# The ends of a state-space scan loop: two of four step-size tiles made inside the loop, and a new order at the loop's first and last pairs

## The chip, the cores and the metric

The kernel runs on one NeuronCore of a Trainium2 chip. The metric is device time in microseconds. Engines are named as in the profile: PE is TensorE (PEld its weight loads), DVE is VectorE, ACT is ScalarE, POOL is GpSimd, SP issues the DMAs.

## The reference, cut to what matters

The reference is a small network of four layers on an input of 2 x 16 x 16 tokens with 64 channels. Each layer is a mixer and a mixture of experts. The change touches only the first layer's mixer, a four-directional selective scan over 256 positions (SEQ) in each of two images:

```python
delta = jax.nn.softplus(dts + dt_b[:, None, :, None])      # step sizes, 4 directions x 128 channels
A = -jnp.exp(A_logs)
def step(h, inp):                                          # 16 states a channel
    dt, bt, ct, ut = inp
    h = jnp.exp(dt[..., None] * A) * h + (dt * ut)[..., None] * bt[:, None, :]
    return (h, jnp.einsum('bdn,bn->bd', h, ct))
# ys of the 4 directions (rows, rows reversed, columns, columns reversed) + Dv * u are summed
y = y * jax.nn.silu(z);  return y @ out_proj_w
```

Behind it come a layer norm, the experts, a neighbourhood attention, an involution and so on, which the change leaves alone.

## The kernel before, in words

The kernel is written by hand for each engine: five instruction streams, in a fixed order, that meet at semaphores. Nothing is scheduled by a planner; an engine that waits holds up all that stands behind in its stream.

**Tiles.** A tile k (0 to 3) is one direction: 128 channels x 512 positions (both images). Channel states are laid out 8 channels x 16 states on 128 partitions, so a direction has 16 such tiles, worked as 8 pairs; the loop runs over 32 pairs (PAIRS), pair i being of direction i // 8. One pair is 128 partitions x 1024 float32.

**Step sizes of tile k.** `dts(k)` (PE, L749) multiplies the input by the folded weights into PSUM bank k. ACT takes Abs, Exp(-|x|) and Relu of it (L540 to L543). The softplus is then relu + log(1 + z), with the log made in two parts, above and below a bound: DVE's `bounded` (three tensor_scalar, L1312, L1316, L1321), ACT's log (L520), `lost` (L354) and `log1p` (L360) on POOL (tile 0's log1p on DVE), `small_log` (L1333; for tile 0 two instructions, L1337 and L1339, for the others one behind ACT's `square`, L525), `delta_log` (L1347), `delta` (L1353) and `delta_u` (delta times u, L345).

**A pair i in the loop.**
- PE: `spread_delta(i)` (L811) spreads delta over the 16 states into decay banks 0 and 1 or 2 and 3; `spread_input(i)` (L817) spreads delta x u into banks 4 and 5. Both use 32 rows of the array at a time. `spread_ahead(i + 1)` in iteration i waits for times-B of i + 1 and for scan i - 1, then does `spread_delta(i + 1)` and `spread_input(i + 2)`.
- ACT: `decays(i)` (L536), two exponentials in place in PSUM.
- DVE: `times_b(i)` (L1378), banks 4 and 5 times B into `states[i % 4]`, and the scan (L1391). The order is times-B 0, then in iteration i times-B i + 1, scan i, and after it the small steps for coming tiles.
- POOL: `hc(i)`, states times C (L452), for all pairs but the last, which DVE makes (L1412).
- PE: `sum_states(q)` (L841) sums the states of pairs 2q and 2q + 1 into bank 6, in iterations 3, 5, and so on behind the spreads.

B and C of a direction are made by `bc_mm` (PE, L754) into bank 7 and `bc_copy` (ACT, L516). `bias_blocks` (L789) are small matmuls for the next stage, in iterations 22 to 25.

**Ahead of the loop** PE does dts 0 and 1, the reversal of the input (`rev`, L759), `bc_mm(0)`, dts 2 and 3, the skip term into bank 6 (`d_mix`, L768), `bc_mm(1)`, four warming matmuls on zeros (L703), then the first spreads. ACT prepares all four tiles there, with pair 0's decays between tiles 2 and 3.

**Behind the loop** PE does six warming matmuls and the last state sum; DVE gates bank 6 (L1418) and the projection follows.

The SP queue holds the loads of weights and is not touched.

## Time and profile before

| | us |
|---|---|
| median of 3 runs | 340.89 |
| lowest, highest run | 339.46, 342.68 |
| profiled execution: span from first to last instruction | 344.4 |
| busy in that span: PE, DVE, ACT, POOL | 279.1, 249.1, 152.3, 128.5 |
| mean granted TensorE clock | 0.857 |

The profiled execution is one execution of its own, and its span is somewhat longer than the timed runs; of its own time only the span is known. All positions below are microseconds from the start of the span. Matmuls of float32 appear as two instructions each. The granted clock is 1.00 at 2.4 GHz and 0.50 at 1.2 GHz. What stands in square brackets behind a row is the idle time of the engine just ahead of it and what ended it.

### The profile page before, as it was taken

The page shows a single profiled execution, that of the slowest core. Times are in us where ns is not written, and L with a number is a line of the kernel's source. Part 1 is how long each engine was busy: PE and PEld are TensorE (multiplying, and loading weights), DVE is VectorE, ACT ScalarE, POOL GpSimd, SP SyncE. Part 2 cuts the span into 40 slices and gives each one's busy share as a digit, 9 for nine tenths or more (in the row PEclk, how much of TensorE's full clock was granted, in tenths as well). Part 3 has the DMA queues.
Part 4 walks back from the last instruction along what each step waited for, and adds up shares of the span by engine and source line. Part 5 has one row for each costly group of instructions (what it writes and reads, how often), then busy time and mean ns, then how long its engine had stood idle before and what let it go on. Part 6 is the DMA issues. An engine that isn't in the chain of part 4 may idle for free.

```text
span 344.4 us, 4760 instructions
## 1 busy us (share of the span) xinstructions
PE 279.1 (81%) x1632; PEld 139.5 (41%) x1632; DVE 249.1 (72%) x654; ACT 152.3 (44%) x339; POOL 128.5 (37%) x97
## 2 busy tenths in 40 slices
PE   7998675665469589699899689999988999699692
PEld 3433111111111134113455357775546554556461
DVE  2228899999999997986775745645767465876854
ACT  1058534434424422432657345857641647224240
POOL 4003467796898986782400023420000000102002
PEclk9999559889956965858999757999999999769898
DMA  6980000000000000003100000000000000000000
GB/s 210 347 332 1 0 3 0 0 0 3 0 0 1 2 0 0 0 2 135 49 2 0 3 1 0 2 3 2 0 0 3 1 2 0 0 3 0 10 0 8
DMA packets 5289, 9.67 MB, mean 28 GB/s; under 512 B 2721, under 2 KB 3425, under 8 KB 5010
## 3 DMA queue, kind: packets, MB, share of 16 engines
q1 hardware_dynamic: 5266, 9.37, 7.9%
q8 instruction: 13, 0.21, 0.3%
q14 instruction: 10, 0.08, 0.1%
HBM read 9.24 MB, written 0.13 MB: 27 GB/s over the span
## 4 chain that ended last, share of the span: by engine, by line
PE 57%; DVE 29%; issue 8%; ACT 3%; POOL 2%; DVEq 0%; POOLq 0%; ACTq 0%
DVE arena L1391 10%; PE ps L811 6%; PE ps L912 6%; PE ps L897 5%; DVE arena L1378 5%; PE ps L1154 4%; PE ps L703 4%; PE ps L841 4%; DVE x L1519 3%; PE ps L1052 2%; PE ps L742 2%; PE ps L1065 2%; PE ps L709 2%; PE ps L1038 2%; PE ps L927 2%
## 5 line engine op out<-in xcount | busy, mean ns | idle before, releaser
L452 POOL TENSOR_TENSOR arena<-arena 128x1024 f32<-128x1024 f32 x31 | 77.0, 2484 | 26.0 <-DVE arena L1391 23.7
L811 PE MATMUL ps<-arena 32*128 32x510 f32 x128 | 49.8, 862 | 35.5 <-DVE arena L1378 34.0
L1391 DVE TENSOR_TENSOR_SCAN arena<-ps,arena 128x1024 f32<-128x1024 f32 x32 | 73.1, 2284 | 1.7 <-ACT ps L536 1.6
L536 ACT ACTIVATE ps<-ps,aneg 128x510 f32<-128x510 f32 x64 | 39.6, 656 | 73.4 <-PE ps L811 73.4
L817 PE MATMUL ps<-arena 32*128 32x512 f32 x128 | 49.8, 864 | 1.3 <-DVE arena L1378 1.3
L416 POOL TENSOR_TENSOR rstd<-ve,mhalf 128x2 f32<-128x2 f32 (+1 forms) x14 | 10.6, 756 | 107.1 <-DVE ve L1255 98.3
L1378 DVE TENSOR_TENSOR arena<-ps,arena 128x1024 f32<-128x1024 f32 x32 | 39.0, 1217 | 5.8 <-PE ps L817 5.4
L811 PEld LDWEIGHTS ps<-arena 32*128 32x128 f32 x128 | 12.8, 240 | 66.8 <-DVE arena L1378 47.0
L581 ACT ACTIVATE arena<-ps,cols 128x256 f32<-128x256 f32 x64 | 25.5, 473 | 14.0 <-PE ps L899 13.3
L1519 DVE SCALAR_TENSOR_TENSOR x<-ps,ww,x 128x64 f32<-128x64 f32 x88 | 18.2, 277 | 9.1 <-PE ps L927 8.9
L841 PE MATMUL ps<-arena,c 128*32 128x512 f32 x128 | 24.6, 829 | 0.0
L1154 PE MATMUL ps<-xt,arena 64*128 64x256 f32 x64 | 20.6, 464 | 3.4 <-DVE arena L1725 3.3
L1155 PE MATMUL ps<-xt,arena 64*128 64x256 f32 x64 | 20.6, 464 | 0.0
L686 ACT ACTIVATE arena<-ps 128x512 f32<-128x512 f32 x16 | 9.6, 597 | 24.7 <-PE ps L1155 24.7
L475 POOL TENSOR_TENSOR arena<-arena,rrec 128x704 f32<-128x704 f32 x8 | 10.9, 1359 | 22.3 <-DVE rrec L1646 22.3
L897 PE MATMUL ps<-xt,arena 64*128 64x256 f32 x64 | 18.6, 405 | 0.4 <-ACT arena L581 0.2
L899 PE MATMUL ps<-xt,arena 64*128 64x256 f32 x64 | 18.6, 405 | 0.0
L912 PE MATMUL ps<-arena 128*64 128x256 f32 x128 | 17.3, 392 | 0.0
L637 ACT ACTIVATE arena<-arena,nmx 128x176 f32<-128x176 f32 x32 | 13.7, 430 | 5.5 <-DVE nmx L1641 5.5
L1154 PEld LDWEIGHTS ps<-xt,arena 64*128 64x128 f32 x64 | 13.1, 220 | 7.3 <-DVE arena L1725 4.5
L581 ACT ACTIVATE arena<-ps,b1f 128x256 f32<-128x256 f32 x32 | 12.7, 474 | 6.3 <-PE ps L899 5.9
L1725 DVE TENSOR_TENSOR arena<-arena,ps 128x512 f32<-128x512 f32 x16 | 11.0, 685 | 5.9 <-ACT arena L686 5.9
(217 smaller groups left out, 539.6 us busy)
## 6 DMA issues: line engine op xcount, KB each, us to landing
arena<-in_w SPq DMA_DIRECT2D x5, 512.0 KB, 5.2
bias<-in_rpb SPq DMA_DIRECT2D x1, 1408.0 KB, 7.4
w<-in_w SPq DMA_DIRECT2D x2, 512.0 KB, 5.4
arena<-in_w SPq DMA_DIRECT2D x1, 1024.0 KB, 10.8
arena<-in_w_conv SPq DMA_DIRECT2D x1, 576.0 KB, 3.7
c<-in_c SPq DMA_DIRECT2D x1, 512.0 KB, 4.5
w_bc<-in_w_bc SPq DMA_DIRECT2D x1, 512.0 KB, 6.1
arena<-in_spread SPq DMA_DIRECT2D x1, 256.0 KB, 6.2
```

Source lines behind the costliest of these rows:

```text
L452: pool.tensor_tensor(hc[:, i % HC_SLOTS], states[i % 4], c_all, ALU.mult).then_inc(hc_done, 1)
L536: act.activation(a, a, ACT.Exp, scale=aneg[:, q:q + 1]).then_inc(exp_done, 1)
L581: act.activation(hid[:, j], bank(1 + j % 4)[:, 0:HALF], func, bias=b1).then_inc(hid_ready, 1)
L811: pe.matmul(dst, spread[rows_, m], src, start=True, stop=True).then_inc(dspread, 1)
L817: last = pe.matmul(bank(4 + s), spread[rows_, m], dd[rows_, i // PAIRS_PER_DIR, 1], start=True, stop=True)
L841: last = pe.matmul(ps[32 * g:32 * g + 32, 6, :], state_sum[:, m], hc[:, i % HC_SLOTS, s], start=False, stop=(q == PAIRS // 2 - 1), skip_gr ...
L897: pe.matmul(bank(1 + j % 4)[:, 0:HALF], w1_block(f, blk), img(xt[0:CH], im), start=True, stop=True)\
L912: last = pe.matmul(ps[o:o + CH, 5 + p % 2, 0:HALF], w2[f][:, 4 * p + 2 * (q % 2) + q // 2], hid[:, j], start=(q < 2), stop=(q >= 2), skip_ ...
L1154: pe.matmul(bank(a)[:, o:o + HALF], w1_block(3, j), img(xt[0:CH], im), start=True, stop=True)
L1378: dve.tensor_tensor(states[i % 4], ps[:, 4:6, :], b_all, ALU.mult).then_inc(mul_done, 1)
L1391: dve.tensor_tensor_scan(h, decay_banks(i).rearrange("p s l -> p (s l)"), h, 0.0, ALU.mult, ALU.add).then_inc(scan_done, 1)
L1519: ins = dve.scalar_tensor_tensor(out=out_[:, t], in0=in0, scalar=w, in1=out_[:, t], op0=ALU.mult, op1=ALU.add)
```

## The change

- **Tiles 2 and 3 move into the loop.** Their dts are in PE's iterations 2 and 10 (into bank 7), ACT's three operations (`prepared`) in iterations 3 and 11. Tiles 0 and 1 use banks 5 and 6. The B and C products of the next direction move from iterations 2 and 4 of a direction to 4 and 5, their copies from 3 and 5 to 5 and 6. The small steps of tiles 1 to 3 stand one or two iterations later.
- **Tile 0.** `lost(0)` goes from POOL to DVE, `small_log(0)` becomes one instruction behind a `square(0)` on ACT. Tile 1's `bounded` goes from ahead of times-B 0 to behind times-B 1, its `lost` and `log1p` on POOL to behind hc 0 and hc 1.
- **First pairs.** DVE: times-B 0, scan 0, times-B 1, `bounded(1)`, times-B 2, scan 1, then as before. PE: spreads of 0, `spread_delta(1)` without a wait, `spread_input(1)`, the skip term (`mixed_input`), `spread_input(2)`, then the reversal, and on with `spread_ahead(2)`. All four decay banks' first columns are zeroed ahead of the step sizes.
- **Last pairs.** `spread_delta(31)` stands ahead of the state sum of pairs 26 and 27. DVE makes the last product in two halves, one an image, and PE sums the last pair by halves. Pair 30 is summed ahead of them.
- `w_fdt` gets a buffer of its own.

The diff, cut:

```diff
 WARM_NORM = 17
 
 
-BOUNDED_AT = {4: 2, 11: 3}
-LOST_AT = {7: 2, 14: 3}
-LOG_AT = {7: 2, 14: 3}
-LOG1P_AT = {8: 2, 15: 3}
-SMALL_LOG_AT = {0: 1, 8: 2, 15: 3}
-DELTA_LOG_AT = {1: 1, 9: 2, 16: 3}
-DELTA_AT = {2: 1, 10: 2, 17: 3}
-DELTA_U_AT = {12: 2, 19: 3}
+DTS_AT = {2: 2, 10: 3}
+PREPARED_AT = {3: 2, 11: 3}
+BC_AT, BC_COPY_AT = (4, 5), (5, 6)
+BOUNDED_AT = {5: 2, 13: 3}
+LOST_AT = {0: 1, 8: 2, 16: 3}
+LOG_AT = {2: 1, 8: 2, 16: 3}
+LOG1P_AT = {1: 1, 9: 2, 17: 3}
+SMALL_LOG_AT = {2: 1, 9: 2, 17: 3}
...
         w_conv = view(27392, TAPS * INNER).rearrange("p (s c) -> p s c", s=TAPS)
         w_xdt = view(28544, DIRS * P)[0:RANK].rearrange("p (k c) -> p k c", k=DIRS)
         w_dt = view(29056, DIRS * P)[0:RANK].rearrange("p (k c) -> p k c", k=DIRS)
...
                 q, h = divmod(n, HEADS)
                 pool.tensor_tensor(bias[:, q, h], bias[:, q, h], window[:, q], ALU.add).then_inc(bias_ready, 1)
 
-            lost(pool, 0)
-            lost(pool, 1)
-            log1p(pool, 1)
-
...
                     act.activation(a, a, ACT.Exp, scale=aneg[:, q:q + 1]).then_inc(exp_done, 1)
...
-                if k == 1:
-                    act.wait_ge(prep_ps, 1)
-                    act.activation(aexp[:], bank(4)[:, 0:64], ACT.Exp).then_inc(aexp_ready, 1)
-                    bc_copy(0)
-                    act.wait_ge(aexp_ready, 1)
-                    act.activation(aneg[:], aexp[:], ACT.Copy, scale=-1.0).then_inc(aneg_ready, 1)
-                    act.wait_ge(rev_ps, 1)
-                    act.activation(u[:, 1], bank(5), ACT.Copy).then_inc(u_back_ready, 1)
-                if k == 2:
-                    decays(0)
-
-            bc_copy(1)
-            log_of(1)
+                act.activation(dd[:, k, 0], delta_bank(k), ACT.Relu, bias=col("dt_b", k)).then_inc(relu_ready, 1)
+
+            prepared(0)
+            log_of(0)
+            act.wait_ge(zeroed, 2)
+            act.activation(log_at[:], log_from[:], ACT.Ln, bias=1.0).then_inc(log_at_ready, 1)
             act.wait_ge(half_c1_set, 1)
-            square(1)
-            act.activation(grid(u[:, 3]), columns_first(u[:, 1]), ACT.Copy).then_inc(u_back_ready, 1)
-            for i in range(1, PAIRS):
+            square(0)
+            act.wait_ge(prep_ps, 1)
+            act.activation(aexp[:], bank(4)[:, 0:64], ACT.Exp).then_inc(aexp_ready, 1)
+            bc_copy(0)
+            act.wait_ge(aexp_ready, 1)
+            act.activation(aneg[:], aexp[:], ACT.Copy, scale=-1.0).then_inc(aneg_ready, 1)
+            prepared(1)
+
+            for i in range(PAIRS):
                 k, ii = divmod(i, PAIRS_PER_DIR)
                 decays(i)
+                if i == 0:
+                    bc_copy(1)
+                if i == 1:
+                    act.wait_ge(rev_ps, 1)
+                    act.activation(u[:, 1], bank(7), ACT.Copy).then_inc(u_back_ready, 1)
                 if i in LOG_AT:
                     log_of(LOG_AT[i])
                     square(LOG_AT[i])
-                if k < DIRS - 1 and ii in (3, 5):
-                    bc_copy(2 * (k + 1) + (ii == 5))
+                if i in PREPARED_AT:
+                    prepared(PREPARED_AT[i])
+                if i == 4:
+                    act.wait_ge(u_back_ready, 1)
+                    act.activation(grid(u[:, 3]), columns_first(u[:, 1]), ACT.Copy).then_inc(u_back_ready, 1)
+                if k < DIRS - 1 and ii in BC_COPY_AT:
+                    bc_copy(2 * (k + 1) + BC_COPY_AT.index(ii))
 
...
             def dts(k):
-                pe.matmul(bank(k), w_fdt[:, k], u[:, 0 if k < 2 else 2], start=True, stop=True).then_inc(dts_ps, 1)
+                if k >= 2:
+                    pe.wait_ge(bc_sb, 2 * k - 2)
+                    pe.wait_ge(u_back_ready, 1)
+                    pe.wait_ge(u_ready, 1)
+                pe.matmul(delta_bank(k), w_fdt[:, k], u[:, 0 if k < 2 else 2], start=True, stop=True).then_inc(dts_ps, 1)
 
...
+                if q in (2, 4):
+                    pe.wait_ge(relu_ready, q // 2 + 2)
...
             dts(0)
             dts(1)
-            got("c32")
-            pe.matmul(bank(5), anti, u[:, 0], start=True, stop=True).then_inc(rev_ps, 1)
             got("w_bc")
             bc_mm(0)
-            pe.wait_ge(u_ready, 1)
-            pe.wait_ge(zs_ready, 1)
-            dts(2)
-            dts(3)
-            pe.wait_ge(diag_ready, 1)
-            for a in range(2):
-                pe.matmul(bank(6), d_mix[:, a], u[:, 2 * a], start=(a == 0), stop=False, skip_group_check=True)
-            bc_mm(1)
+
+            def mixed_input():
+
+                pe.wait_ge(diag_ready, 1)
+                pe.wait_ge(u_ready, 1)
+                pe.wait_ge(relu_ready, 2)
+                for a in range(2):
+                    pe.matmul(bank(6), d_mix[:, a], u[:, 2 * a], start=(a == 0), stop=False, skip_group_check=True)
+
+            def reversed_input():
+
+                pe.wait_ge(bc_sb, 2)
+                pe.matmul(bank(7), anti, u[:, 0], start=True, stop=True).then_inc(rev_ps, 1)
 
 
...
                     delta_known(i + 1, 1)
                     pe.wait_ge(mul_done, i + 1)
-                if i == 1:
-                    pe.wait_ge(first_cols_zero, 2)
-                else:
-                    pe.wait_ge(scan_done, i - 1)
+                pe.wait_ge(scan_done, i - 1)
                 spread_delta(i)
...
-                    if i < PAIRS - HC_ON_DVE:
-                        pe.wait_ge(hc_done, i + 1)
-                    else:
-                        pe.wait_ge(hc_last, i + 1 - (PAIRS - HC_ON_DVE))
+                    if i == PAIRS - 1:
+                        continue
+                    pe.wait_ge(hc_done, i + 1)
                     for s, (g, m) in enumerate(pair_tiles[i]):
...
+                if q < PAIRS // 2 - 1:
+                    last.then_inc(sum_done, 1)
+
+            def sum_last():
+
+                i = PAIRS - 1
+                for im in range(IMAGES):
+                    pe.wait_ge(hc_last, im + 1)
+                    for s, (g, m) in enumerate(pair_tiles[i]):
+                        last = pe.matmul(img(ps[32 * g:32 * g + 32, 6, :], im), state_sum[:, m], img(hc[:, i % HC_SLOTS, s], im),
+                                         start=False, stop=True, skip_group_check=True)
                 last.then_inc(sum_done, 1)
 
             got("spread")
...
-            pe.wait_ge(first_cols_zero, 1)
+            bc_mm(1)
+            pe.wait_ge(first_cols_zero, 2)
             delta_known(0, 0)
             spread_delta(0)
             delta_known(0, 1)
-            pe.wait_ge(u_back_ready, 1)
             spread_input(0)
+            spread_delta(1)
             pe.wait_ge(mul_done, 1)
             spread_input(1)
-            got("c16")
+            got("c16", "c32")
+            mixed_input()
+            pe.wait_ge(mul_done, 2)
+            spread_input(2)
             for i in range(PAIRS):
                 k, ii = divmod(i, PAIRS_PER_DIR)
-                if i + 1 < PAIRS:
+                if 0 < i < PAIRS - 1:
                     spread_ahead(i + 1)
-                if i >= 3 and i % 2:
+                if i == 0:
+                    reversed_input()
+                if i in DTS_AT:
+                    dts(DTS_AT[i])
+                if i >= 3 and i % 2 and i != PAIRS - 3:
                     sum_states((i - 3) // 2)
-                if k < DIRS - 1 and ii in (2, 4):
-                    bc_mm(2 * (k + 1) + (ii == 4))
+                if i == PAIRS - 2:
+                    sum_states((i - 4) // 2)
+                if k < DIRS - 1 and ii in BC_AT:
...
             pe.wait_ge(mul_done, PAIRS)
             keep_warm(6, 5)
             sum_states(PAIRS // 2 - 1)
+            sum_last()
...
 
-                if k:
-                    dve.wait_ge(square_ready, k)
-                    link(dve.scalar_tensor_tensor(out=z_[k], in0=z_[k], scalar=LOG_C0 - LOG_C1 ** 2 / 4, in1=zmin[k],
-                                                  op0=ALU.add, op1=ALU.mult))
-                    return
-                dve.wait_ge(zmin_ready, 1)
-                link(dve.scalar_tensor_tensor(out=z_[0], in0=zmin[0], scalar=LOG_C1, in1=zmin[0],
-                                              op0=ALU.add, op1=ALU.mult))
-                link(dve.scalar_tensor_tensor(out=z_[0], in0=z_[0], scalar=LOG_C0, in1=zmin[0],
+                dve.wait_ge(square_ready, k + 1)
+                link(dve.scalar_tensor_tensor(out=z_[k], in0=z_[k], scalar=LOG_C0 - LOG_C1 ** 2 / 4, in1=zmin[k],
...
+            dve.wait_ge(zs_ready, 1)
+            zero_first_columns(0)
+            zero_first_columns(1)
             bounded(0)
+            lost(dve, 0)
+            log1p(dve, 0)
             small_log(0)
-            dve.wait_ge(relu_ready, 2)
-            zero_first_columns(0)
-            log1p(dve, 0)
             delta_log(0)
             delta(0)
             delta_u(dve, 0)
-            bounded(1)
...
                 k, ii = divmod(i, PAIRS_PER_DIR)
-                if i + 1 < PAIRS:
+                if 0 < i < PAIRS - 1:
                     times_b(i + 1)
-                if i == 0:
-                    dve.wait_ge(relu_ready, DIRS)
-                    zero_first_columns(1)
                 dve.wait_ge(mul_done, i + 1)
                 dve.wait_ge(exp_done, 2 * i + 2)
                 h = states[i % 4].rearrange("p s l -> p (s l)")
                 dve.tensor_tensor_scan(h, decay_banks(i).rearrange("p s l -> p (s l)"), h,
                                        0.0, ALU.mult, ALU.add).then_inc(scan_done, 1)
+                if i == 0:
+                    times_b(1)
+                    bounded(1)
...
-                if i == 3:
+                if i == 5:
                     delta_u(dve, 1)
 
             c_all = bc[:, DIRS - 1, 1].unsqueeze(1).to_broadcast([P, 2, 2 * SEQ])
-            for i in range(PAIRS - HC_ON_DVE, PAIRS):
-                dve.wait_ge(scan_done, i + 1)
-                dve.wait_ge(sum_done, (i - HC_SLOTS) // 2 + 1)
-                dve.tensor_tensor(hc[:, i % HC_SLOTS], states[i % 4], c_all, ALU.mult).then_inc(hc_last, 1)
+            dve.wait_ge(scan_done, PAIRS)
+            dve.wait_ge(sum_done, (PAIRS - 1 - HC_SLOTS) // 2 + 1)
+            for im in range(IMAGES):
+                cc = slice(HALF * im, HALF * im + HALF)
+                dve.tensor_tensor(hc[:, (PAIRS - 1) % HC_SLOTS, :, cc], states[(PAIRS - 1) % 4][:, :, cc],
+                                  c_all[:, :, cc], ALU.mult).then_inc(hc_last, 1)
```

## Rows read from the trace of the kernel before

**Rows 1.** Stretches: us, busy (instructions) of PE, PEld, DVE, ACT, POOL, clock, DMA.

```profile
32.71:157.98 125.27, 88.48 (x422) 24.68 (x422) 118.45 (x83) 51.59 (x85) 94.32 (x55) 0.74 0.00 1
...
159.13:344.40 185.27, 159.84 (x1133) 102.02 (x1133) 117.83 (x537) 88.27 (x233) 28.37 (x29) 0.91 0.03 10
```

**Rows 2.** Waits, 30 to 160 us: total us, times, longest.

```profile
DVE arena L1378 <- PE ps L817: 5.4, 4, 2.2
...
DVE arena L1391 <- ACT ps L536: 1.6, 1, 1.6
```

**Rows 3.** Timeline (start us, us, what), step sizes of tile 0.

```profile
25.71 1.65 POOL L354 TENSOR_TENSOR arena<-arena 128x512 f32<-128x512 f32 x1 [19.76 <-DVE arena L1321]
...
26.26 1.65 DVE L1339 SCALAR_TENSOR_TENSOR arena<-arena 128x512 f32<-128x512 f32 x1
...
28.03 0.69 DVE L360 TENSOR_TENSOR arena<-arena 128x512 f32<-128x512 f32 x1
...
29.54 0.69 DVE L1353 SCALAR_TENSOR_TENSOR arena<-arena 128x512 f32<-128x512 f32 x1
...
30.68 1.12 PE L811 MATMUL ps<-arena 32*128 32x510 f32 x4
```

**Rows 4.** Timeline of the first pairs, DVE and PE.

```profile
32.71 1.23 DVE L1378 TENSOR_TENSOR arena<-ps,arena 128x1024 f32<-128x1024 f32 x1 [0.74 <-PE ps L817]
...
33.99 2.08 PE L817 MATMUL ps<-arena 32*128 32x512 f32 x4 [1.33 <-DVE arena L1378]
...
39.46 0.67 DVE L1333 SCALAR_TENSOR_TENSOR z<-z,xn 128x512 f32<-128x512 f32 x1
...
41.30 2.28 DVE L1391 TENSOR_TENSOR_SCAN arena<-ps,arena 128x1024 f32<-128x1024 f32 x1
```

**Rows 5.** Timeline: DVE beside POOL, at tile 2 and in the next stage.

```profile
68.79 1.27 POOL L354 TENSOR_TENSOR z<-arena,z 128x512 f32<-128x512 f32 x1
...
69.55 1.05 DVE L1333 SCALAR_TENSOR_TENSOR z<-z,xt 128x512 f32<-128x512 f32 x1
...
163.47 0.60 DVE L1265 TENSOR_SCALAR xn<-x,mv,rstd 128x128 f32<-128x128 f32 x2
...
166.65 1.80 POOL L466 MEMSET arena<- 88x2048 f32 x1
...
167.79 1.38 DVE L1265 TENSOR_SCALAR xn<-x,mv,rstd 128x128 f32<-128x128 f32 x2
```

**Rows 6.** Groups by line, 20 to 160 us: busy us, mean ns.

```profile
L536 ACT ACTIVATE ps<-ps,aneg 128x510 f32<-128x510 f32 x64 | 39.6, 656 | 73.4 <-PE ps L811 73.4
...
L543 ACT ACTIVATE arena<-ps,cols 128x512 f32<-128x512 f32 x4 | 2.7, 670 | 0.0
...
L1312 DVE TENSOR_SCALAR arena<-z 128x512 f32<-128x512 f32 x3 | 1.2, 409 | 0.0
...
L768 PE MATMUL ps<-arena 128*128 128x512 f32 x4 | 1.9, 592 | 0.0
```

**Rows 7.** Stretches: first pairs, bias blocks, last pairs.

```profile
34.00:38.00 4.00, 2.51 (x8) 0.97 (x12) 1.89 (x3) 3.55 (x6) 1.28 (x1) 0.50 0.00 0
...
126.00:134.00 8.00, 8.00 (x36) 4.59 (x32) 5.80 (x4) 2.11 (x4) 5.53 (x4) 0.50 0.00 0
...
146.60:157.00 10.40, 9.90 (x34) 2.16 (x34) 8.70 (x6) 5.13 (x9) 8.07 (x6) 0.51 0.01 2
```

**Rows 8.** Timeline at the last pairs.

```profile
149.12 1.94 PE L841 MATMUL ps<-arena,c 128*32 128x512 f32 x8
...
150.99 2.07 PE L811 MATMUL ps<-arena 32*128 32x510 f32 x4
...
152.98 2.35 POOL L452 TENSOR_TENSOR arena<-arena 128x1024 f32<-128x1024 f32 x1 [0.72 <-DVE arena L1391]
...
154.43 2.29 DVE L1391 TENSOR_TENSOR_SCAN arena<-ps,arena 128x1024 f32<-128x1024 f32 x1 [1.59 <-ACT ps L536]
...
157.23 1.86 PE L841 MATMUL ps<-arena,c 128*32 128x512 f32 x8
```

29 lines of the change are left out of this document (15 added, 14 removed).

## The prediction

> **What bounds the kernel now.** I read the table of stretches first. The scan loop with its ends, 32.71 to 157.98 us, is 125 us of the 344.4 us span, and in it VectorE (DVE) is busy 118.45 us, PE 88 us, GpSimd (POOL) 94 us and ScalarE (ACT) 52 us [rows 1]: DVE bounds the loop. The stage behind it, 159.13 to 344.40, holds none of the changed code, and I give it no gain. The list of waits then says what idles DVE in the loop: 5.4 us in 4 waits of times-B for a spread by PE, and 1.6 us in one wait of a scan for ACT [rows 2]. So about 7 us are to be had there at most; all else is DVE's own work, which an order of instructions can't shorten. Where they lie is read from the timeline: 2.2 us between times-B 0 and 1, 2.2 us and 0.3 us near 131 to 135 us, 1.6 us ahead of the last scan.
>
> **Head, first part: the step sizes of tile 0.** Before, `lost(0)` is made by POOL in 1.65 us while DVE's second instruction of `small_log(0)` runs 1.65 us beside it, though the same kind takes 0.67 us elsewhere; only at 28.03 does `log1p(0)` follow, and `delta(0)` ends at 29.54 + 0.69 = 30.23 us [rows 3, 4]. After, the last of the three bounds still ends near 25.63; `lost(0)` (0.69, as L360) and `log1p(0)` (0.69) follow on DVE, so log1p starts at 26.3; one `small_log` of 0.67 instead of two stands between it and the unchanged rest of 2.20 us (28.03 to 30.23). That gives 26.3 + 2.2 + 0.7 = 29.2 us, 1.0 earlier. ACT's added `square(0)` (some 0.7 us, as its other passes over 512 columns [rows 6]) starts near 25.6, behind the log of tile 0, and is done ahead of its use near 27.0: nothing. PE, whose four warming matmuls let the spread start at 30.68 only, 0.45 us behind `delta(0)`, now has them ahead (they wait for `aexp`, near 26.5 on ACT, and end near 27.8, with `bc_mm(1)` 0.9 us behind them): the spread starts at 29.2 and times-B 0 at 32.71 - 1.5 = 31.2 us. Tiles 2 and 3 (a dts, and three ACT operations of 0.67 us each [rows 6], 2.0 us) leave this place, but stood behind what the end waits for: removing them gives nothing in itself.
>
> **Head, second part: the first scan.** From 31.2: times-B 0 to 32.4, scan 0 to 34.7 (2.28), in what was DVE's wait for PE. `spread_input(1)` begins at 32.5 and takes about 1.1 us at full clock and 2.08 at half [rows 3, 4], so it is ready for times-B 1, 34.6 to 35.8, either way. Now `bounded(1)`, which stood in idle time before, costs three times 0.41, about 1.1 us with their overlaps [rows 6], and it meets POOL: `hc(0)` starts when scan 0 ends and lasts 2.4 us (34.8 to 37.1). DVE's rows show that its SBUF-only instructions wait for a running POOL one: two L1265 take 0.60 us alone and 1.38 us under a POOL memset, and `small_log(2)` takes 1.05 us for 0.67 when it begins under POOL's L354 [rows 5]. So `bounded(1)` ends at 38.2, not 36.9. The price of that is between 0 and 1.3 us, and I take 1.3, as the two rows are of the same kinds. The Trainium skill (SBUF — State Buffer, "Who interferes with whom") speaks against this place too: it says that such a VectorE instruction and a GpSimd one share a port pair as an exclusive lock. By that rule the head is 1.3 us worse than by plain durations; the trace agrees, with its 1.38 us.
> Then times-B 2 runs 38.2 to 39.4, if `spread_input(2)` is there. It waits for times-B 1 (35.8) and stands behind `mixed_input`, four full-array instructions, 1.88 us at full clock [rows 6]. At full clock these end at 35.4 and the spread at 36.9, in time; if the clock falls near 34, as it did before (0.50 in 34 to 38 [rows 7]), three of the four take 0.85 us each, they end at 36.5 and the spread at 38.6, 0.4 us late. Scan 1 starts at 39.3 to 39.7 instead of 41.30 [rows 4]; I take 39.5: 1.8 us earlier. But `small_log(1)` (0.67, less an overlap of 0.06) is still to come, and under POOL's `log1p(1)` costs some 0.4 more. Head: 1.8 - 0.6 - 0.4 = 0.8 us gained.
>
> **The loop.** PE gets `reversed_input`, two dts (0.9 us each at full clock); ACT gets 2.0 us at pairs 3 and 11. ACT uses two decays of 0.66 us [rows 6] in a period of about 3.7 (118.45 us of DVE over 32 pairs), so it holds 2.0 more, and the next decays are due only when DVE has done a times-B and a scan. Behind ACT's new wait for `rev_ps` stand the copy and decays 2; the reversal comes near 37.8, decays 2 not before 40.6. On PE, pair 5 of each direction now has both spreads, a state sum and a `bc_mm`: 1.1 + 1.1 + 0.9 = 3.1 us at full clock (spread rows, where the two of a pair interleave, come to 1.2), within the period; 5.7 us at half (2.1 + 1.9 + 1.7), 2.0 over it. Of these DVE feels half: a spread starts when a times-B ends, its decays end 1.1 + 1.3 us later, and the scan that reads them comes 2.28 + 1.23 later, so 1.1 us is slack. I take 0.2 us lost over the three; the ends are 0 and 4. POOL's lost, log1p and delta_u keep their distance of one pair; nothing there. The two stalls at 131 to 135 us lie in a stretch in which PE ran bias blocks at half clock [rows 7]; the change leaves their code, so 0, and their whole 2.5 us either way belongs to the range.
>
> **The tail.** The scan of pair 31 waits 1.59 us for ACT, since PE does a state sum from 149.12 and `spread_delta(31)` only from 150.99 [rows 8]. After, that spread starts when scan 29 is done (149.3), and scan 31 follows scan 30 at 152.8: 1.6 us earlier. DVE's last product then ends at 156.4. But PE is late next. Before, it worked without a wait from 149.12 to 157.23, where the last pair of sums began; the same work in another order, 8.1 us, now starts at 149.3 and ends at 157.4, and with 1.9 us of sums the end is 159.3, no better than before (157.23 + 1.86 = 159.09). With the clock risen one stretch earlier, pair 30 waits for POOL (`hc(30)` ends at 155.33), 156.2, and the last sum ends 157.3: 1.8 gained. The halves save 0.4 us where DVE is last, for a second fixed cost of 0.1. Bounds 0 and 1.8; I take 0.8, near the middle: the clock was 0.51 in 146.6 to 157 [rows 7], PE being busy 9.9 us of it, and the change moves one spread and one sum closer together, no more.
> **Sum.** 0.8 + 0.8 - 0.2 = 1.4 us off the profiled 344.4: 343.0. That span is above all three timed runs (339.46 to 342.68); taken off their median of 340.89 it is **339.5 us**.
>
> **Rivals.** (a) *The clock falls earlier at the head.* At half clock from 32 us on, `spread_input(1)` ends at 34.6, `mixed_input` at 38.4 (twice 1.88) and `spread_input(2)` at 40.5; scan 1 starts at 41.7. The head turns from 0.8 gained to 41.3 - 41.7 - 1.0 = 1.4 lost: 339.5 + 2.2 = 341.7. For it: PE now idles near 25 for some 2 us and near 29 for 0.5, where it had dts and reversal before, and before the clock was 0.50 in 34 to 38 [rows 7], behind 3 us of nothing but spreads and a wait. Against: with 22 to 24.5 and the warming matmuls the work is still dense up to 28.7, and what follows has the dense `mixed_input`. Chance 0.25. The Trainium skill (TensorE: Matmul & The Clock Gate, "What's actually happening") has the throttled clock as the default and recent activity as what lifts it; by that rule the idle near 25 brings (a), and 341.7. The trace before agrees so far as the 0.50 behind a stretch with little work goes. (b) *More is gained:* no lock of `bounded(1)` (1.1 to 1.3), the tail's 1.8 (1.0 more) and half of the 2.5 us near 131, PE's clock being up there: 339.5 - 1.2 - 1.0 - 1.2 = 336.1; the first two alone give 337.3. Chance 0.2. (c) *Slower:* the crowded queue of PE. At half clock its pairs 5, 13 and 21 run 2.0 us over the period, and the dts at 2 and 10 (1.7 us each there) follow on spreads that leave no room; where that uses up the 1 us of slack ahead of the next scan, DVE waits 1 to 2 us each time. Five such places, at 1 us each, and a head and tail of nothing: 340.9 + 5 = 345.9; with the gains of the ends 344.5. It decides from four of the five on. Against: the clock is full in most of these stretches, and DVE bore PE's half clock elsewhere with no more than the 5.4 us of [rows 2] in the whole loop. Chance 0.1. The forecast, 0.45, covers 338.2 to 340.7.
>
> **Chances.** About 1% (3.4 us: 337.5 and 344.3) is what a measurement of this kernel can tell. Faster by over 1%: (b) and a little of the forecast's edge, 0.23. Slower by over 1%: most of (c), 0.09. Within: 0.68. The range takes the forecast, (a), and (b) but for its far half: 336.8 to 342.3.
>
> **What would show it.** Right: times-B 0 near 31.2 us; scan 0 ahead of times-B 1; `bounded(1)`'s first instruction near 1.7 us long instead of 0.42, ending with `hc(0)`; scan 1 near 39.5; scan 31 without a wait for ACT; the last wait before the gating on PE. Wrong: a wait of times-B 2 for PE past 39 us (a); waits of DVE for PE or ACT behind pairs 5, 13, 21 (c); `bounded(1)` at 0.42 each (b).

## The result, and the profile after

The changed kernel takes 342.68 us (median of 22 runs, 339.95 to 348.73) against 339.91 us (22 runs, 336.34 to 348.20) for the kernel before, timed in turn with it on the same chips. The ratio is 1.0086, with a 95% interval of 1.0059 to 1.0114: 0.9% slower, 2.9 us, clear of zero though within the 1% that the prediction named as what can be told. The time lies above the range of 336.8 to 342.3, and the difference has the opposite sign to the forecast. Every kernel here, the one before too, has executions some per cent longer at a lower granted clock, which the ratios leave out and the medians don't; of the profiled executions only those of before_again, b1_two_small, a1_bounded6, a9_masks and a11_masks_back_tail are of the shorter kind, and those of the kernel before and of the changed one are both of the longer.

The profiled execution of the changed kernel has a span of 344.8 us at a mean clock of 0.849, that of before 344.4 at 0.857. These two spans can't be set against each other: behind the gate, in a stage whose code is the same, the time was 187.8 us after and 185.3 before, and between 179.1 and 189.2 in the other profiles of this study. So 2.6 of the 3.8 us by which the changed kernel's profile is longer, counted from the common starting point named next, lie behind the gate, and the comparison that follows leaves them out. The traces are compared by positions up to the gate (first DVE instruction of L1450 after, L1418 before), counted from the start of the three bounds of tile 0 (L1347 at 21.16 us after, L1312 at 24.53 before; the input's load landed within 0.1 us of the same time, at 3.0 us, but in the execution before PE's first matmuls ran slower: the two on the input took 2.05 and 1.91 us there, 1.10 and 1.02 after).

The stretches of the changed kernel, from times-B 0 to the end of the last product, then from the gate to the end, then the head behind times-B 0. The columns are as in [rows 1]:

```profile
27.99:156.13 128.14, 92.92 (x430) 24.76 (x432) 124.87 (x86) 54.15 (x89) 94.89 (x55) 0.75 0.00 1
156.97:344.80 187.83, 162.36 (x1133) 103.72 (x1133) 117.73 (x537) 88.17 (x233) 28.38 (x29) 0.89 0.03 10
28.80:35.60 6.80, 6.33 (x10) 2.18 (x12) 6.15 (x6) 1.23 (x3) 2.88 (x2) 0.50 0.00 0
```

Its waits of DVE from 30 to 160 us (total us, times, longest):

```profile
DVE arena L1408 <- PE ps L834: 2.7, 5, 1.5
...
DVE arena L1418 <- ACT ps L539: 0.2, 1, 0.2
```

The first row is to be read against the first of [rows 1]. The stretch grew from 125.27 to 128.14 us, and in it DVE's idle time shrank, from 6.8 us to 3.3; the waits for PE and ACT did shrink, as the second view shows beside [rows 2]. But DVE's busy time grew from 118.45 to 124.87, by 6.4 us, and the work added there (the three instructions of `bounded(1)`, and one more for the product that is now halved) would take some 1.3 us at the duration of [rows 6]. Most of the rest is in DVE instructions that have become longer. The timeline shows the two largest, `bounded(1)` at the head and `delta_u(1)` (L350) behind scan 5:

```profile
25.13 0.69 DVE L1382 SCALAR_TENSOR_TENSOR arena<-arena 128x512 f32<-128x512 f32 x1
...
27.99 1.23 DVE L1408 TENSOR_TENSOR arena<-ps,arena 128x1024 f32<-128x1024 f32 x1 [1.44 <-PE ps L834]
29.25 2.29 DVE L1418 TENSOR_TENSOR_SCAN arena<-ps,arena 128x1024 f32<-128x1024 f32 x1
31.27 3.78 PE L781 MATMUL ps<-arena 128*128 128x512 f32 x4
31.46 1.20 DVE L1408 TENSOR_TENSOR arena<-ps,arena 128x1024 f32<-128x1024 f32 x1
31.69 2.35 POOL L457 TENSOR_TENSOR arena<-arena 128x1024 f32<-128x1024 f32 x1 [25.63 <-DVE arena L1418]
32.57 1.75 DVE L1347 TENSOR_SCALAR arena<-z 128x512 f32<-128x512 f32 x1
36.45 1.22 DVE L1408 TENSOR_TENSOR arena<-ps,arena 128x1024 f32<-128x1024 f32 x1 [1.46 <-PE ps L834]
37.59 2.28 DVE L1418 TENSOR_TENSOR_SCAN arena<-ps,arena 128x1024 f32<-128x1024 f32 x1
...
53.17 2.28 DVE L1418 TENSOR_TENSOR_SCAN arena<-ps,arena 128x1024 f32<-128x1024 f32 x1
55.37 0.40 DVE L1347 TENSOR_SCALAR arena<-z 128x512 f32<-128x512 f32 x1
55.59 2.37 POOL L457 TENSOR_TENSOR arena<-arena 128x1024 f32<-128x1024 f32 x1 [1.27 <-PE ps L854]
55.69 2.83 DVE L350 TENSOR_TENSOR arena<-arena 128x512 f32<-128x512 f32 x1
58.44 1.21 DVE L1408 TENSOR_TENSOR arena<-ps,arena 128x1024 f32<-128x1024 f32 x1
59.57 2.27 DVE L1418 TENSOR_TENSOR_SCAN arena<-ps,arena 128x1024 f32<-128x1024 f32 x1
```

L1347 took 1.75 us for 0.41 and ended 0.28 us behind POOL's `hc(0)`, much as forecast. L350 took 2.83 us where the same instruction takes 0.66 in a run below. It ended 0.56 us behind the POOL instruction beside it, `hc(5)` (55.59 + 2.37 = 57.96; 58.52), so it stood until that one had ended and then ran for about its own duration: scan 6 starts 6.40 us behind scan 5, where the distances beside it are 3.9 and 3.65. This was not in the prediction. No wait shows it: the engine is booked as busy.

### The profile page after: what moved, and what is told of

It is laid out like the page before. It is cut to its first block, busy times and chain, and to the rows that moved or that the text cites. A ratio compares the mean times of both kernels' runs of the same rounds, so it can differ in the third digit from the quotient of the medians.

```text
span 344.8 us, 4770 instructions
## 1 busy us (share of the span) xinstructions
PE 278.2 (81%) x1636; PEld 137.9 (40%) x1636; DVE 253.4 (73%) x655; ACT 153.0 (44%) x340; POOL 126.8 (37%) x96
## 4 chain that ended last, share of the span: by engine, by line
PE 52%; DVE 31%; issue 8%; ACT 5%; POOL 2%; DMA 1%; POOLq 0%; DVEq 0%; ACTq 0%
DVE arena L1418 10%; PE ps L828 7%; DVE arena L1408 6%; PE ps L947 6%; PE ps L932 5%; PE ps L854 4%; DVE x L1551 3%; PE ps L1189 3%; PE ps L1087 2%; PE ps L750 2%; PE ps L711 2%; PE ps L1100 2%; PE ps L1073 2%; PE ps L717 2%; PE ps L962 2%
## 5 line engine op out<-in xcount | busy, mean ns | idle before, releaser
L828 PE MATMUL ps<-arena 32*128 32x510 f32 x128 | 47.9, 838 | 34.8 <-DVE arena L1408 28.4
L1418 DVE TENSOR_TENSOR_SCAN arena<-ps,arena 128x1024 f32<-128x1024 f32 x32 | 72.9, 2279 | 0.3 <-ACT ps L539 0.2
L539 ACT ACTIVATE ps<-ps,aneg 128x510 f32<-128x510 f32 x64 | 39.5, 656 | 63.1 <-PE ps L828 63.1
L834 PE MATMUL ps<-arena 32*128 32x512 f32 x128 | 48.7, 845 | 1.3 <-DVE arena L1408 1.3
L1189 PE MATMUL ps<-xt,arena 64*128 64x256 f32 x64 | 20.0, 453 | 3.0 <-DVE arena L1757 3.0
L1190 PE MATMUL ps<-xt,arena 64*128 64x256 f32 x64 | 20.0, 453 | 0.0
L480 POOL TENSOR_TENSOR arena<-arena,rrec 128x704 f32<-128x704 f32 x8 | 10.9, 1360 | 22.3 <-DVE rrec L1678 22.3
L932 PE MATMUL ps<-xt,arena 64*128 64x256 f32 x64 | 18.6, 405 | 0.3 <-ACT arena L589 0.2
L934 PE MATMUL ps<-xt,arena 64*128 64x256 f32 x64 | 18.6, 405 | 0.0
L1669 DVE CUSTOM_DVE_ANT_0 arena<-ps,bias 128x176 f32<-128x176 f32 x32 | 9.0, 335 | 8.9 <-PE ps L1073 8.9
```

The source lines that it names most:

```text
L539: act.activation(a, a, ACT.Exp, scale=aneg[:, q:q + 1]).then_inc(exp_done, 1)
L828: pe.matmul(dst, spread[rows_, m], src, start=True, stop=True).then_inc(dspread, 1)
L834: last = pe.matmul(bank(4 + s), spread[rows_, m], dd[rows_, i // PAIRS_PER_DIR, 1], start=True, stop=True)
L932: pe.matmul(bank(1 + j % 4)[:, 0:HALF], w1_block(f, blk), img(xt[0:CH], im), start=True, stop=True)\
L1189: pe.matmul(bank(a)[:, o:o + HALF], w1_block(3, j), img(xt[0:CH], im), start=True, stop=True)
L1418: dve.tensor_tensor_scan(h, decay_banks(i).rearrange("p s l -> p (s l)"), h, 0.0, ALU.mult, ALU.add).then_inc(scan_done, 1)
```

## The experiments

The positions, in us from the start of the bounds of tile 0, each worked out from the timeline of one profiled execution. In the column "behind the gate" stands what follows it, whose code no kernel changes.

| kernel | scan 0 | scan 1 | scan 5 | scan 6 | scan 8 | scan 22 | scan 29 | scan 31 | gate | behind the gate |
|---|---|---|---|---|---|---|---|---|---|---|
| before | 12.73 | 16.77 | 32.22 | 35.86 | 42.82 | 95.53 | 122.43 | 129.90 | 134.60 | 185.3 |
| before, again | 11.78 | 15.82 | 31.27 | 34.92 | 42.15 | 94.37 | 123.28 | 129.60 | 134.30 | 179.1 |
| b1_two_small | 11.78 | 15.82 | 33.81 | 37.46 | 44.58 | 97.26 | 121.91 | 128.03 | 133.02 | 181.8 |
| b1_again | 11.78 | 15.82 | 33.77 | 37.42 | 44.42 | 97.09 | 121.71 | 129.17 | 133.87 | 186.2 |
| after | 8.09 | 16.43 | 32.01 | 38.41 | 45.71 | 99.70 | 124.72 | 130.50 | 135.81 | 187.8 |
| a1_bounded6 | 8.09 | 15.08 | 30.65 | 34.57 | 41.86 | 95.94 | 121.93 | 127.71 | 132.91 | 183.2 |
| a9_masks | 8.09 | 14.89 | 30.45 | 34.36 | 41.66 | 94.44 | 120.91 | 126.68 | 131.89 | 180.6 |
| a11_masks_back_tail | 8.08 | 16.41 | 31.99 | 35.90 | 43.20 | 96.09 | 121.20 | 126.71 | 131.54 | 181.8 |
| a13_only_masks | 8.09 | 14.89 | 30.44 | 36.84 | 44.13 | 97.07 | 121.66 | 127.16 | 132.00 | 189.2 |

**One pair's collision, undone and made alone.** In the changed kernel two DVE instructions that touch no PSUM stand behind scan 5: the first of `bounded_from(2)` and `delta_u(1)`. One kernel moves the first to pair 6, with nothing else changed:

```
 # a1_bounded6, on the changed kernel
-BOUNDED_AT = {5: 2, 13: 3}
+BOUNDED_AT = {6: 2, 13: 3}
```

> The changed kernel with BOUNDED_AT = {6: 2, 13: 3}: bounded_from(2) one scan later, so that no scan has two small VectorE instructions behind it. Theory A (VectorE waits for GpSimd at pair 5): delta_u(1) goes back to 0.7 us, the scans 5 and 6 stand 3.9 us apart instead of 6.4, and the kernel gains 2.3 us over the changed one: ratio to before 1.0086 - 0.0068 = 1.002. Theory B (PE's queue at pair 5): the scans stay 6.4 us apart and the ratio stays at 1.0086.

The other takes the kernel before, where each of them has a pair to itself, and puts them together behind scan 4. It was run twice (b1_again is the same kernel):

```
 # b1_two_small and b1_again, on the kernel before
-                if i == 3:
+                if i == 4:
                     delta_u(dve, 1)
```

> The kernel before with one edit: delta_u(1) stands behind scan 4, where bounded_from(2) already stands, instead of alone behind scan 3. No work is added. Theory A (a second small VectorE instruction behind one scan finds GpSimd's product running and waits for its end, 2.35 us): delta_u(1) takes 2.8 us instead of 0.67, the scan behind it starts 2.2 us later, and the kernel is 2.2 us slower than before, 0.6%. Theory B (what the changed kernel lost at pair 5 comes from PE, which has both spreads, a state sum and a product for B or C there): this kernel has no such pair, delta_u(1) keeps 0.67 us and the time stays within 0.3 us of before.

> The kernel before with delta_u(1) behind scan 4 beside bounded_from(2), a second time, since the first run had an interval of half a per cent either way though its trace showed scan 5 starting 2.5 us late. If those 2.5 us reach the end of the kernel, the ratio is 1.005 to 1.007; if they are given back at PE's waits behind pair 24 (in the first run's trace the wait of 2.2 us at the bias blocks was not there), it is 1.000 to 1.003.

The timeline of b1_two_small (L345 is `delta_u` there, L452 the POOL product, L1391 the scan):

```profile
51.53 2.29 DVE L1391 TENSOR_TENSOR_SCAN arena<-ps,arena 128x1024 f32<-128x1024 f32 x1
...
53.73 0.40 DVE L1312 TENSOR_SCALAR arena<-z 128x512 f32<-128x512 f32 x1
...
53.96 2.37 POOL L452 TENSOR_TENSOR arena<-arena 128x1024 f32<-128x1024 f32 x1 [1.41 <-DVE arena L1391]
54.05 2.83 DVE L345 TENSOR_TENSOR arena<-arena 128x512 f32<-128x512 f32 x1
```

And that of a1_bounded6 on DVE:

```profile
54.91 2.28 DVE L1418 TENSOR_TENSOR_SCAN arena<-ps,arena 128x1024 f32<-128x1024 f32 x1
57.11 0.66 DVE L350 TENSOR_TENSOR arena<-arena 128x512 f32<-128x512 f32 x1
57.69 1.21 DVE L1408 TENSOR_TENSOR arena<-ps,arena 128x1024 f32<-128x1024 f32 x1
58.83 2.27 DVE L1418 TENSOR_TENSOR_SCAN arena<-ps,arena 128x1024 f32<-128x1024 f32 x1
```

Alone behind its scan, `delta_u` took 0.66 us and the next scan came 3.92 us later. With `bounded_from` ahead of it, in the kernel before as in the changed one, it took 2.83 us and the next scan came 6.41 and 6.40 us later. The reason can be read from the starts: POOL's product is released by the end of the scan and starts about 0.2 us behind DVE's next instruction (53.73 and 53.96). The first small instruction is in by then; the second meets the running POOL one, stands until it has ended, and then runs. All six executions here of a kernel with both in one pair have the 2.83 us, and none of the other eight has such an instruction. So each pair has room for one such instruction, and none for two: 2.5 us in the trace.

What it is worth in the timed runs isn't settled. b1_two_small came to 1.0005 (0.9951 to 1.0058) and b1_again to 1.0048 (1.0001 to 1.0095): 0.2 and 1.6 us by the ratios, for the same kernel, and the whole 2.5 (1.0074) lies inside the second interval and outside the first. The table shows a possible reason for less. b1_two_small is 2.5 us behind the second execution of the kernel before at scan 5, 2.9 at scan 22, and ahead of both executions of before at scan 29, as is b1_again: the wait of 2.2 us that both executions of before have in the stretch of the bias blocks (below) is missing in both of these. a1_bounded6 was expected at 1.002 and came to 1.0075 (1.0033 to 1.0116), hardly less than the change itself, though its profile is 3.8 us ahead of that of the change at scan 22, 1.4 of it from the head. So pair 5 alone isn't the whole.

**PE's crowded queue (rival (c)).** The second `bc_mm` of each direction goes from pair 5 to pair 6, so that PE's queue at pair 5 holds only spreads and a state sum:

```
 # a4_bc_apart, on the changed kernel
-BC_AT, BC_COPY_AT = (4, 5), (5, 6)
+BC_AT, BC_COPY_AT = (4, 6), (5, 7)
```

> The changed kernel with the second product for B and C of a direction in iteration 6 instead of 5 and its copy in 7 instead of 6, so that PE never has a state sum and such a product in one iteration. Theory A (port of VectorE and GpSimd): nothing changes, ratio to before 1.0086 within 0.002. Theory B (PE's crowded queue, my rival c): 1 to 2 us come back at each of three places, ratio 0.995 to 1.000.

The distance of scans 5 and 6 stayed, at 6.39 us. The time is no guide here: 6 runs from 336.55 to 348.70 us, too scattered for a ratio. By the trace, rival (c) is not what happened at pair 5.

**The head.** The expectation below blames the full-array `mixed_input`, which stands ahead of `spread_input(2)` in PE's queue; both it and the collision of `bounded(1)` are moved out of the way:

```
 # a3_back_mix_late, on the changed kernel: PE; DVE
-            mixed_input()
             pe.wait_ge(mul_done, 2)
             spread_input(2)
+            mixed_input()
 ...
+            bounded(1)
 ...
                 if i == 0:
                     times_b(1)
-                    bounded(1)
```

> The changed kernel with bounded(1) back ahead of times-B 0 and the skip term's matmuls behind spread_input(2) instead of ahead of it. Theory C (the head's gain went to two things: bounded_from(1), which waits 1.3 us for GpSimd's first product, and spread_input(2), which waits 3.8 us for the skip term at half clock): scan 1 follows scan 0 after 5.7 us instead of 8.3, bounded(1) lies in VectorE's wait of 1.4 us ahead of times-B 0 and costs nothing, and the kernel gains 2.6 us over the changed one: ratio 1.001. Theory D (the head is bound by PE's spreads whatever stands between them): the distance of scans 0 and 1 falls by under 1 us and the ratio stays above 1.006.

Scans 0 and 1 were 6.80 us apart, not the 5.7 that theory C needs, and scans 1 and 2 were 5.30 apart instead of the 3.32 of the changed kernel: `mixed_input`, 3.26 us at half clock, now stood ahead of the next pair's spreads, and times-B 3 waited 1.78 us for PE. The delay had moved on by one pair. Time 1.0125 (1.0037 to 1.0213), from 6 runs: no gain over the change from this other order on PE.

**The kernel before once more.**

> The kernel before, unchanged, timed against itself. It tells how far two kernels with the same time can come apart here, and gives a second profile of the kernel before. Ratio 1.000 within its interval; the wait of 2.2 us at the bias blocks and that of 1.6 us ahead of the last scan are at other places or gone, if they hang on where PE's clock stands and not on the code.

Ratio 0.9989 (0.9938 to 1.0040), span 334.5 us against 344.4, of which 6.2 us lie behind the gate. Its gate has nearly the same position, 134.30 against 134.60. The wait at the bias blocks was there again, and once more behind it; the wait of the last scan for ACT was 0.67 us, not 1.59. It was 0.26 in b1_two_small and 1.59 in b1_again.

**The masks.** In a1_bounded6 one place was still slow, pair 18, where DVE's `delta_log(3)` (L1376) waits for POOL's `log1p(3)` (L365). The change moved `lost` and `log1p` of tile 3 to pairs 16 and 17, and `MASK_AT`, the list of pairs at which POOL adds the window's mask to a part of the bias (L445), still has 16 and 17 in it. The next kernel keeps pair 5 repaired and moves the masks off POOL's full pairs:

```
 # a9_masks, on a1_bounded6
-MASK_AT = [9, 10, 16, 17, 18] + list(range(20, 31))
+MASK_AT = [10, 11, 13, 14, 18, 19] + list(range(21, 31))
```

> The changed kernel with bounded_from(2) one scan later (as in the run of that edit alone) and the bias masks of GpSimd moved off the pairs 16 and 17, where they now stand beside lost(3) and log1p(3): MASK_AT = [10, 11, 13, 14, 18, 19] and 21 to 30. Theory E (GpSimd's log1p(3) comes late behind a mask, and delta_log(3) waits for it): the distance of scans 18 and 19 falls from 4.9 to 4.1 us, those of 13 to 14 and 17 to 18 by 0.2 each, 1.2 us in all, ratio to before 1.0015. Rival (this distance comes from PE or ACT, which got tile 3's work): nothing changes.

The timeline on POOL and DVE in the changed kernel:

```profile
103.67 0.55 POOL L445 TENSOR_TENSOR bias<-bias,c 128x176 f32<-128x176 f32 x1
104.18 2.80 POOL L457 TENSOR_TENSOR arena<-arena 128x1024 f32<-128x1024 f32 x1
106.94 1.26 POOL L365 TENSOR_TENSOR z<-z,arena 128x512 f32<-128x512 f32 x1
...
108.23 1.02 DVE L1376 SCALAR_TENSOR_TENSOR z<-z,log_at,arena 128x512 f32<-128x512 f32 x1
```

In a1_bounded6:

```profile
106.05 1.26 POOL L365 TENSOR_TENSOR z<-z,arena 128x512 f32<-128x512 f32 x1
...
107.34 1.03 DVE L1376 SCALAR_TENSOR_TENSOR z<-z,log_at,arena 128x512 f32<-128x512 f32 x1 [0.52 <-POOL z L365]
```

And in a9_masks:

```profile
104.88 1.26 POOL L365 TENSOR_TENSOR z<-z,arena 128x512 f32<-128x512 f32 x1
106.18 0.75 DVE L1376 SCALAR_TENSOR_TENSOR z<-z,log_at,arena 128x512 f32<-128x512 f32 x1
```

With the masks on its path, POOL's log1p ends at 107.31 in a1_bounded6, where DVE has stood waiting for it for 0.52 us, and the `delta_log` behind it takes 1.03 us instead of 0.75, since the next POOL instruction, a mask's, starts beside it. Scans 18 and 19 were 4.37 us apart in the changed kernel, 4.89 in a1_bounded6, 4.09 in a9_masks. The 0.2 us expected at each of two other places didn't come: 13 and 14 stayed at 4.03, and 17 and 18 went from 4.17 to 4.43, while 16 and 17 went from 3.56 to 3.31. From scan 8 to scan 24 the times are 60.88, 60.70 and 59.68 us in these three, and 59.62 and 59.12 in the two executions of before: 1.0 to 1.2 us in all.

a9_masks ran at 1.0001 (0.9946 to 1.0056) of the kernel before. With pair 5 and the masks repaired, and head, loop order and tail as the change has them, the loss is gone: the interval lies below that of the change (1.0059 to 1.0114). The masks alone:

```
 # a13_only_masks, on the changed kernel
-MASK_AT = [9, 10, 16, 17, 18] + list(range(20, 31))
+MASK_AT = [10, 11, 13, 14, 18, 19] + list(range(21, 31))
```

> The changed kernel with the bias masks on GpSimd moved and nothing else. If what the change lost is 2.5 us at pair 5 and 1.2 us at the masks, each by itself, this one gains 1.2 us over the changed kernel: ratio 1.0086 - 0.0035 = 1.005, the distance of scans 5 and 6 stays at 6.4 us and that of 18 and 19 is 4.1.

The trace did as expected (scans 18 and 19 4.09 us apart, scans 5 and 6 still 6.40), the time did not: 1.0122 (1.0067 to 1.0177). With the four corners

| | masks as in the change | masks moved |
|---|---|---|
| pair 5 as in the change | 1.0086 | 1.0122 |
| pair 5 repaired | 1.0075 | 1.0001 |

the mean effect of pair 5 is (0.0011 + 0.0121) / 2 = 0.66%, that of the masks (-0.0036 + 0.0074) / 2 = 0.19%. One corner's interval is 0.3 to 0.55% to each side, so only the diagonal can be relied on: both together 0.85%, 2.9 us, give or take 0.6%.

**`bounded(1)` in its old place.** It goes back ahead of times-B 0, where POOL is idle:

```
 # a10_masks_back, on a9_masks
+            bounded(1)
 ...
                 if i == 0:
                     times_b(1)
-                    bounded(1)
```

> As the kernel with both edits (bounded_from(2) later, masks moved), and bounded(1) back ahead of times-B 0, where VectorE waits 1.4 us for PE. Theory C (the 1.3 us that bounded_from(1) waits for GpSimd, and its own 1.1 us, lie on the path): scan 1 starts up to 2.4 us earlier, ratio 0.995. Theory D (spread_input(2) behind the skip term is as late): scan 1 starts at most 0.5 us earlier where the clock is half, and the ratio stays within 0.002 of that of the two edits.

Its timeline at the head (DVE line numbers are one up here):

```profile
29.70 0.42 DVE L1347 TENSOR_SCALAR arena<-z 128x512 f32<-128x512 f32 x1
...
31.22 1.22 DVE L1409 TENSOR_TENSOR arena<-ps,arena 128x1024 f32<-128x1024 f32 x1 [0.43 <-PE ps L834]
...
33.56 3.67 PE L781 MATMUL ps<-arena 128*128 128x512 f32 x4
...
37.16 1.13 PE L834 MATMUL ps<-arena 32*128 32x512 f32 x4
...
38.33 1.23 DVE L1409 TENSOR_TENSOR arena<-ps,arena 128x1024 f32<-128x1024 f32 x1 [2.45 <-PE ps L834]
```

The long instruction is gone (0.42 us for 1.75), and nothing is won: scans 0 and 1 are 6.99 us apart, and 6.80 in a9_masks. Times-B 2 now waits 2.45 us for `spread_input(2)`, which stands behind a `mixed_input` of 3.67 us. In a9_masks the same place looked so:

```profile
33.24 1.98 PE L781 MATMUL ps<-arena 128*128 128x512 f32 x4
...
35.49 1.75 DVE L1347 TENSOR_SCALAR arena<-z 128x512 f32<-128x512 f32 x1
35.62 1.13 PE L834 MATMUL ps<-arena 32*128 32x512 f32 x4 [0.40 <-DVE arena L1408]
...
37.83 1.21 DVE L1408 TENSOR_TENSOR arena<-ps,arena 128x1024 f32<-128x1024 f32 x1
```

There `mixed_input` ran at full clock, the spread was done at 36.75, and `bounded(1)` was last, at 37.90. So two limits of nearly one size lie on this place: the collision where PE's clock is up, PE's queue where it is down. The fall of the clock doesn't come from the removal: in a1_bounded6 and a4_bc_apart, which have `bounded(1)` where the change puts it, the clock fell at the same place, some 9.3 us behind the start of the bounds, and scan 1 stands at 15.08 and 15.05, exactly as here (15.08) and in a12_bias_even (15.05), which have it back. With the clock falling there, `bounded(1)` costs no more in its new place than in its old one. Ratio 0.9996 (0.9951 to 1.0042); theory C, which wanted 0.995, isn't borne out.

**The tail of before.** On top of it, the last state sums, spreads and the last product are put back to what the kernel before has (the sum ahead of the last spread, the product and its sum whole):

```
 # a11_masks_back_tail, on a10_masks_back
-                if i >= 3 and i % 2 and i != PAIRS - 3:
+                if i >= 3 and i % 2:
                     sum_states((i - 3) // 2)
-                if i == PAIRS - 2:
-                    sum_states((i - 4) // 2)
 ...
-            for im in range(IMAGES):
-                cc = slice(HALF * im, HALF * im + HALF)
-                dve.tensor_tensor(hc[:, (PAIRS - 1) % HC_SLOTS, :, cc], states[(PAIRS - 1) % 4][:, :, cc],
-                                  c_all[:, :, cc], ALU.mult).then_inc(hc_last, 1)
+            dve.tensor_tensor(hc[:, (PAIRS - 1) % HC_SLOTS], states[(PAIRS - 1) % 4], c_all, ALU.mult).then_inc(hc_last, 1)
```

> As the kernel before it in this list (three edits), with the tail of the kernel before: the state sum ahead of the last spread, the last product and its sum in one piece. My forecast had 0.8 us for the new tail, between 0 and 1.8. Theory F (it holds 0.4 to 1.8): this one is that much slower, ratio up by 0.001 to 0.005. Theory G (the halves meet GpSimd's product of pair 30 and give back what the earlier scan 31 gained): within 0.3 us of the same.

0.9998 (0.9952 to 1.0045) against 0.9996 with the new tail: no difference, as theory G had it. From scan 29 to the gate the old tail took 10.3 to 12.2 us in seven profiles, 11.2 in the mean, and the new one 10.3 to 11.1 in seven, 10.9 in the mean. Two of the seven old ones have bias blocks elsewhere (below). The tail of the changed kernel:

```profile
151.66 2.29 DVE L1418 TENSOR_TENSOR_SCAN arena<-ps,arena 128x1024 f32<-128x1024 f32 x1 [0.18 <-ACT ps L539]
...
153.98 2.15 DVE L1443 TENSOR_TENSOR arena<-arena 128x512 f32<-128x512 f32 x2
```

Scan 31 no longer waits 1.59 us for ACT as in [rows 8], only 0.18. But the two half products take 2.15 us together, against 1.23 for the whole one before. They start at 153.98, and POOL's `hc(30)`, which had waited for the sum ahead of it, ends at 154.62: 0.64 us of the difference is the wait for it, which a whole product would have had too:

```profile
150.22 3.64 PE L854 MATMUL ps<-arena,c 128*32 128x512 f32 x16
...
152.27 2.35 POOL L457 TENSOR_TENSOR arena<-arena 128x1024 f32<-128x1024 f32 x1 [1.08 <-PE ps L854]
```

**The stretch of the bias blocks.** The kernel before has a distance of 5.7 us from scan 24 to 25 in both its executions, and in the second one more, from 26 to 27. This is the timeline of PE and DVE between scans 24 and 25 (122.36 and 128.07), in before_again:

```profile
120.97 1.94 PE L841 MATMUL ps<-arena,c 128*32 128x512 f32 x8
...
122.84 1.86 PE L789 MATMUL ps<-cols,w 64*128 64x1 f32 x8
124.63 1.22 PE L811 MATMUL ps<-arena 32*128 32x510 f32 x2
124.64 1.22 PE L817 MATMUL ps<-arena 32*128 32x512 f32 x2
...
126.83 1.23 DVE L1378 TENSOR_TENSOR arena<-ps,arena 128x1024 f32<-128x1024 f32 x1 [2.18 <-PE ps L817]
```

A state sum, the weight columns of a bias block (L789) and the spreads of the pair follow on one another at half clock, and DVE stands 2.18 us. Two kernels put the four bias blocks into the even iterations, which have no state sum:

```
 # b2_bias_even, on the kernel before; a12_bias_even, on a11_masks_back_tail
-                if 22 <= i < 26:
-                    bias_blocks(i - 22)
+                if 22 <= i < 30 and i % 2 == 0:
+                    bias_blocks((i - 22) // 2)
```

> The kernel before with the four blocks of small bias matmuls on PE in iterations 22, 24, 26 and 28 instead of 22 to 25, so that none stands in an iteration with a state sum. Theory H (the distance of 5.7 us between two scans, once behind pair 24 to 27 in most traces, comes from spreads, a state sum and a bias block together at half clock, 2.1 + 1.9 + 1.9 = 5.9 us against a period of 3.3): no such distance is left, and the kernel gains up to 2.2 us, ratio 0.994 to 0.997. Rival (it comes from the half clock alone, wherever the blocks stand): the distance stays and the ratio is 1.000.

> The kernel with the two repairs, bounded(1) back and the tail of the kernel before, and the bias blocks in iterations 22, 24, 26 and 28. By theory H it gains up to 2.2 us over the same kernel without that edit (0.9998): ratio 0.994 to 0.997, the fastest so far.

In b2_bias_even DVE's wait there is 0.19 us at the most and no distance from scan 24 on is over 3.71 us:

```profile
121.19 1.23 DVE L1378 TENSOR_TENSOR arena<-ps,arena 128x1024 f32<-128x1024 f32 x1
122.42 2.29 DVE L1391 TENSOR_TENSOR_SCAN arena<-ps,arena 128x1024 f32<-128x1024 f32 x1
124.90 1.22 DVE L1378 TENSOR_TENSOR arena<-ps,arena 128x1024 f32<-128x1024 f32 x1 [0.19 <-PE ps L817]
126.13 2.29 DVE L1391 TENSOR_TENSOR_SCAN arena<-ps,arena 128x1024 f32<-128x1024 f32 x1
```

Scans 24 to 31 took 23.0 us in it, against 27.46 and 28.33 in the two executions of before, and 23.9 in the changed kernel, whose blocks are where they were. That last number is a warning: of the twelve profiles with the blocks in their old place only five have a distance of 5.7 us (before and before_again from 24 to 25, before_again, a1_bounded6, a3_back_mix_late and a9_masks from 26 to 27), and seven have none. Two profiles without one, those of the two kernels here, can be chance, so theory H isn't shown. Timed, b2_bias_even is at 0.9975 (0.9937 to 1.0013) and a12_bias_even at 0.9964 (0.9915 to 1.0012), the lowest of all, at a median of 337.08 us. Neither interval excludes 1: no version shown here beats the kernel before beyond doubt. That the whole 5 us of the traces isn't found in the time may mean that the executions which were timed don't all have these waits.

**What lies behind the gate.** The positions up to the gate don't explain the times. At the gate a1_bounded6 is 1.4 us ahead of before_again, and timed it is 2.5 us slower than before; a13_only_masks is 2.6 ahead of the first profile of before, and timed 4.1 slower. The column "behind the gate" has the missing part. Take the five profiles named with the result. Up to the gate and behind it together, before_again took 313.4 us, b1_two_small 314.8, a1_bounded6 316.1, a9_masks 312.5 and a11_masks_back_tail 313.3: +1.4, +2.7, -0.9 and -0.1, where the times say +0.2, +2.5, 0.0 and -0.1. The code there is the same in all; what differs in the profiles is where PE's clock falls. Seven of the fourteen have a stretch of 17 to 20 us at half clock that begins 34 to 36 us behind the gate, and take 185.3 to 189.2 us there; the other seven don't, and take 179.1 to 183.2. So an edit ahead of the gate may also act by when the stage behind it begins. With one such profile for each kernel, and none of the changed kernel among them, this is neither shown nor excluded.

## Why the prediction was wrong, step by step

**What bounds the kernel:** right, and it gave the error its form. DVE bounds the loop, and about 7 us of idle time were the most to be won; DVE's idle time did fall by 3.5 us. The prediction took DVE's own work as fixed ("which an order of instructions can't shorten"). It didn't ask where the new order would lengthen it, but in one place.

**Head, first part:** `delta(0)` ended 25.13 + 0.69 - 21.16 = 4.66 us behind the bounds' start, where 29.2 - 24.53 = 4.67 was forecast; times-B 0 started at 6.83, forecast 6.67. Right.

**Head, second part:** the collision of `bounded(1)` came at the forecast size (1.75 us, ending just behind `hc(0)`). Scan 1 was forecast at 39.5 - 24.53 = 14.97. Seven of the nine kernels with the new head (four of them with `bounded(1)` back) have it at 14.9 to 15.1, a1_bounded6 and a9_masks among them; two, the profiled execution of the change and a11_masks_back_tail, at 16.4, 1.4 us later. That is rival (a), 0.8 us milder than its price (41.7 - 24.53 = 17.2): in 28.80 to 35.60 the clock was 0.50, `mixed_input` (L781) took 3.78 us, and times-B 2 waited 1.46 us for PE. So the forecast's case and rival (a) both happen, in different executions. The two with the early fall of the clock are also the two in which PE's first matmul on the input took 1.10 us and the bounds started at 21.1; in the seven others it took 2.03 to 2.05 and they started at 22.8 to 24.5. So in these nine executions which case comes goes with something that happened ahead of all changed code. By scan 8, when all small steps of tile 1 are done, a1_bounded6 and a9_masks stand at 41.86 and 41.66 against 42.82 and 42.15: 0.3 to 1.2 us gained, where 0.8 was forecast; the changed kernel's own profile, less the 2.5 us of pair 5, is at 43.2, 0.4 to 1.1 us lost. That the collision costs 1.3 us even where PE's clock is up, as in a9_masks, isn't shown, as no execution without it kept the clock up; in a10_masks_back PE's queue took up the same time without it. The prediction had both limits, at 38.2 and 38.6, and so had the time of scan 1 right.

**The loop, the step that failed:** it costed only PE and ACT, and of the rest it said "POOL's lost, log1p and delta_u keep their distance of one pair; nothing there". Two things were in it.
First, `delta_u(1)` goes to pair 5, where `BOUNDED_AT` puts the first instruction of `bounded_from(2)`. The prediction had the row for this ([rows 5]), and priced the very same meeting at the head 1.3 us, but didn't lay the new tables side by side to find the other place where two such instructions share a pair. Missed: 2.5 us in the trace.
Second, `MASK_AT` isn't in the diff, and so wasn't looked at. A list that stays where it is while its neighbours shift by one or two pairs has moved relative to them: 1.0 to 1.2 us in the trace.
The Trainium skill (SBUF — State Buffer, "Who interferes with whom") states the exclusive lock that this rests on, as cited in the prediction. The traces agree, with 2.83 us for 0.66. They also bear out what it says of a VectorE instruction with at most one input in SBUF, that outside the modes which use two ports it doesn't contend: times-B and the scan, whose other input is in PSUM, keep 1.19 to 1.23 and 2.27 to 2.29 us, beside POOL's products or not.

**PE's crowded queue at pairs 5, 13, 21:** forecast 0.2 us lost. a4_bc_apart gave no change at pair 5, and behind scans 13 and 21 the distances are 4.02 and 3.32 us in the changed kernel and the same in a4_bc_apart, so the small value stands, and rival (c) falls.

**The tail:** mis-sized. 0.8 was taken from bounds of 0 and 1.8; the traces give 0.2 (11.2 us from scan 29 to the gate in the mean of the old tail, 10.9 of the new) and the times 0.9996 against 0.9998. The prediction's reason for the lower bound was right, PE and POOL are late next. Its 1.6 us of wait ahead of scan 31 came from one execution; it was 1.59, 0.67, 0.26 and 1.59 in the four profiles of the kernel before and of the one that differs from it only at pair 4. And DVE's last product meets `hc(30)`, which it didn't ask for: the two halves took 0.9 us more than the whole one before, 0.64 of it that wait; the 0.4 us that the halves should save is not seen.

**The sum.** Forecast: -0.8 - 0.8 + 0.2 = -1.4 us. With what was read: some -0.6 at the head, -0.2 at the tail, +2.5 at pair 5, +1.1 by the masks, together +2.8; timed +2.9. So close an agreement is luck. In the two traces the changed kernel is 4.2 us behind at scan 22 and 1.2 at the gate, since the stretch of the bias blocks stalled DVE in the kernel before (23.9 us from scan 24 to 31 after, 27.46 before) and not in the changed one; the 2.5 us of pair 5 alone came out at 0.2 and 1.6 us in the kernel before; and 2.6 us more lie behind the gate. Shown is that both repairs together remove the loss (1.0001, 0.9996 and 0.9998 in three kernels), and that each removes its own stall in the trace. Open is how the 2.9 us divide, and how much of them the stalls cost where they stand and how much by shifting the stage behind the gate: a13_only_masks, at 1.0122, came 0.7% over what was expected of it. To settle it, many more runs of the four corners would be needed, or several profiles of each, to count how often the waits at scans 24 to 27 occur and to set the times behind the gate side by side. Open too is what makes the clock fall in one execution of the head and not in the next.

## What to carry to other kernels

When steps are shifted in a table, write out for every iteration what each engine now has in it, with the lists that the diff leaves alone, and look for two VectorE instructions without a PSUM operand behind the event that also releases a GpSimd one: the first gets in, the second waits GpSimd out. Such a loss is in no list of waits; it shows as a mean duration that has grown, or as busy time that grows more than the work. And a stall read from one trace is not what the time will show: it may be given back at the next narrow place, and what stands behind it may run at another clock.

## What the runs showed of the hardware that was not expected

An SBUF-only VectorE instruction that starts 0.1 us behind a GpSimd one stands until that one has ended and then runs, and is booked as busy all the while: 2.83 us for 0.66, in six executions of five kernels.

The same code behind the gate took from 179.1 to 189.2 us in different executions, more than any edit here moved. A stretch of 17 to 20 us at half clock that begins 34 to 36 us behind the gate parts them: the profiles of the kernel before, the changed one, b1_again, b2_bias_even, a4_bc_apart, a10_masks_back and a13_only_masks have it, the other seven don't. Spans of single executions could not have settled anything in this case.
